# A recurrent cell on one core: three bf16 parts of h and its weights against one fp32 product in four column tiles

## What is computed

```
fused = sigmoid(concat([x_t, h]) @ w_W + w_b)
hidden_state, output_state = split(fused, 2)
memory_state = x_t @ wx_W + wx_b + hidden_state * (h @ wh_W + wh_b)
h_new = output_state * h + (1 - output_state) * tanh(memory_state)
```

## Time and profile before

| | |
|---|---|
| median of 3 runs | 2035.18 us (2035.16 to 2035.33) |
| the profiled execution | 2036.86 us |
| its span in the trace | 2032.7 us |
| PE busy | 1838.1 us, 90% of the span, 52224 matmul records |
| DVE busy | 1395.7 us, 69% |
| ACT busy | 1076.7 us, 53% |
| POOL busy | 271.1 us, 13% |
| mean granted TensorE clock | 0.997 of full speed |

### The profile page before, as it was taken

One profiled execution on the slowest core, in us unless ns is written; L12 is line 12 of the kernel. 1 busy time (PEld: TensorE's weight loads), 2 busy tenths in 40 slices (PEclk: granted clock), 3 DMA queues, 4 the chain that ended last, 5 costly groups with the idle time before them and its releaser, 6 DMA issues.

```text
span 2032.7 us, 127549 instructions
## 1 busy us (share of the span) xinstructions
PE 1838.1 (90%) x52224; PEld 1646.3 (81%) x52224; DVE 1395.7 (69%) x7191; ACT 1076.7 (53%) x5003; POOL 271.1 (13%) x1284
## 2 busy tenths in 40 slices
PE   5999999999999999999999999999999999999986
PEld 4888888888888888888888888888888888888875
DVE  6666666666666666666666666666666666666666
ACT  4555555555555555555555555555555555555544
POOL 0111111111111111111111111111111111111111
PEclk9999999999999999999999999999999999999989
DMA  5210000000000000000000000000000000000000
GB/s 177 81 45 9 9 9 8 4 8 9 9 9 3 9 8 9 9 8 4 9 8 9 9 5 7 9 8 9 9 3 9 8 9 9 8 4 9 8 9 9
DMA packets 35801, 30.00 MB, mean 15 GB/s; under 512 B 1584, under 2 KB 34352, under 8 KB 35376
## 3 DMA queue, kind: packets, MB, share of 16 engines
q1 hardware_dynamic: 35376, 23.10, 3.5%
HBM read 14.70 MB, written 8.39 MB: 11 GB/s over the span
## 4 chain that ended last, share of the span: by engine, by line
PE 71%; DVE 21%; issue 5%; DMA 1%; SPq 0%; POOL 0%; ACT 0%; POOLq 0%; DVEq 0%
PE ps L218 39%; PE ps L232 33%; DVE m_pre L377 5%; DVE h L397 5%; DVE h L392 5%; DVE h L386 4%; DVE pre_z L373 1%; DMA x_sb<-in_x 1%; PE ps L207 0%; SPq L183 0%; SPq L175 0%; DVE ps L365 0%; SPq L178 0%; POOL y L485 0%; DVE m_add L412 0%
## 5 line engine op out<-in xcount | busy, mean ns | idle before, releaser
L218 PE MATMUL ps<-wh,h 128*24 128x256 bf16 x24576 | 782.6, 276 | 166.3 <-DVE h L397 157.4
L218 PEld LDWEIGHTS ps<-wh,h 128*24 128x24 bf16 x24576 | 648.6, 123 | 261.7 <-DVE h L397 256.5
L232 PEld LDWEIGHTS ps<-h_moving,wh 128*128 128x128 bf16 x24576 | 649.3, 96 | 96.0 <-issue 96.0
L232 PE MATMUL ps<-h_moving,wh 128*128 128x24 bf16 x24576 | 698.9, 173 | 0.0
L365 DVE STREAM_TRANSPOSE ps<-ps 128x128 f32<-128x128 f32 x1024 | 271.2, 310 | 529.2 <-PE ps L218 529.2
L207 PE MATMUL ps<-x_sb,wx 128*128 (+1 forms) x3072 | 460.0, 289 | 22.4 <-DMA wx<-in_w_x 20.3
L306 ACT ACTIVATE m_by<-pre_r 128x32 f32<-128x32 f32 x512 | 133.9, 261 | 631.8 <-DVE pre_r L410 631.8
L301 ACT ACTIVATE h_moving<-h 128x48 bf16<-128x48 bf16 x1024 | 303.9, 297 | 246.3 <-DVE h L397 241.5
L472 POOL COPY m_add<-xg 128x16 f32 (+1 forms) x1024 | 186.6, 218 | 1724.1 <-DVE m_pre L377 1687.3
L207 PEld LDWEIGHTS ps<-x_sb,wx 128*128 128x128 f32 x3072 | 380.9, 192 | 22.8 <-issue 20.3
L290 ACT ACTIVATE h_by<-pre_z 128x16 f32<-128x16 f32 x1024 | 236.7, 231 | 52.4 <-DVE pre_z L373 1.2
(11 more groups left out here) (19 smaller groups left out, 122.3 us busy)
## 6 DMA issues: line engine op xcount, KB each, us to landing
x_sb<-in_x SPq DMA_DIRECT2D x32, 256.0 KB, 3.1
out_h<-y SPq DMA_DIRECT2D x32, 256.0 KB, 2.6
wh_rest<-in_w_h SPq DMA_DIRECT2D x4, 768.0 KB, 11.4
wx<-in_w_x SPq DMA_DIRECT2D x4, 768.0 KB, 11.8
h<-in_h SPq DMA_DIRECT2D x1, 16.0 KB, 1.8
bias_x<-in_b_x SPq DMA_DIRECT2D x1, 6.0 KB, 1.9
bias_h<-in_b_h SPq DMA_DIRECT2D x1, 2.0 KB, 1.7
```

Of the source, the lines that this page charges most:

```text
L218: mm = pe.matmul(ps[Q * j:Q * j + PARTS * B, RM_BANK, 0:RM], parts_of(s - 1 if s else S, k), wh[:, part, k, j * RM:(j + 1) * RM], start=(k ...
L232: mm = pe.matmul(ps[:, Z_BANK + o, ci * SLOTS * B:(ci * SLOTS + PARTS) * B], wh[:, part, k, col:col + P], h_moving[:, k // HC, k % HC, :], ...
```

## The change

h and its weights stay fp32. wh is loaded as it is, in one buffer; the cutting of the weights, the two subtractions on h, h_moving and the reductions over parts go away. Each chunk of h stands as 8 fp32 columns in each of the four column tiles. Two groups of products follow each other: r and m (256 moving columns, PSUM bank 0), then z (128 moving columns, bank 1), both by the one function products. Per step these are 16 + 16 matmuls in place of 48 + 48. z is now turned by a transpose as r and m are (turn_z). The sums of r and z with x's share are plain additions in SBUF; x's share is placed there by one copy on ACT (place_x), two buffers deep. GpSimd adds the bias to hm (hidden), and adds x to h in every step. The order on DVE becomes: both transposes of r and m, sums of r, both m scans, then z. At the start SP loads wx in six parts by unit, then wh, and the x products wait part by part.

```diff
...
-            for k in range(KC // 2):
-                load_wh(k)
+            sp.dma_start(x_sb[:, :, 0:TOK], x_flat[:, :, 0:TOK]).then_inc(x0_loaded, 16)
+            for i in range(WX_PARTS):
+                us = slice(i * UNITS // WX_PARTS, (i + 1) * UNITS // WX_PARTS)
+                sp.dma_start(wx[:, us], w_x[:, us]).then_inc(wx_loaded[i], 16)
+                if i == 0:
+                    sp.dma_start(bias_x[:, :], b_x).then_inc(bias_loaded, 16)
+                    sp.dma_start(bias_h[:, :], b_h).then_inc(bias_loaded, 16)
+                    sp.dma_start(h_0[:, :, :], h0).then_inc(h0_loaded, 16)
             for k in range(KC):
-                sp.dma_start(wx[:, k, :, :], w_x[:, k, :, :]).then_inc(wx_loaded, 16)
-            for k in range(KC // 2, KC):
-                load_wh(k)
+                sp.dma_start(wh[:, k], w_h[:, k]).then_inc(wh_loaded, 16)
+            sp.dma_start(x_sb[:, :, TOK:2 * TOK], x_flat[:, :, TOK:2 * TOK]).then_inc(x_loaded, 16)
...
-            def rm_products(ks, s):
-
...
-                    for part in range(PARTS):
-                        for j in range(TILES):
-                            mm = pe.matmul(ps[Q * j:Q * j + PARTS * B, RM_BANK, 0:RM],
-                                           parts_of(s - 1 if s else S, k),
-                                           wh[:, part, k, j * RM:(j + 1) * RM],
...
-            def z_products(o):
-
-                for ci in range(HC):
...
+            def products(group, half, s):
+
+
+                at, cols, bank = group
+                for k in range(half * HC, (half + 1) * HC):
+                    for j in range(TILES):
+                        mm = pe.matmul(ps[Q * j:Q * j + B, bank, 0:cols], h_of(s - 1 if s else S, k),
+                                       wh[:, k, j, at:at + cols], start=(k == 0), stop=(k == KC - 1),
+                                       tile_position=(0, Q * j))
                 return mm
 
             def step(t0, s):
                 nxt = held(pe, t0 + (s + 1))
                 pe.wait_ge(h_ready[0], nxt)
-                rm_products(range(HC), s)
+                products(RM, 0, s)
                 pe.wait_ge(h_ready[1], nxt)
-                rm_products(range(HC, KC), s).then_inc(rm_done, 1)
-                pe.wait_ge(h_moved, nxt)
-                pe.wait_ge(xz_placed, nxt)
-                for o in range(HALVES):
-                    z_products(o).then_inc(z_done[o], 1)
-
-            pe.wait_ge(x_loaded, 2 * 16)
-            pe.wait_ge(wx_loaded, KC * 16)
+                products(RM, 1, s).then_inc(rm_done, 1)
+                products(Z_ALL, 0, s)
+                products(Z_ALL, 1, s).then_inc(z_done, 1)
+            pe.wait_ge(x0_loaded, 16)
             x_products(x_list, 0, 0)
-            for k in range(KC):
-                pe.wait_ge(first_cut[k], 1)
-                pe.wait_ge(next_cut[k], PARTS - 1)
+            pe.wait_ge(wh_loaded, KC * 16)
             pe.wait_ge(ps_cleared, 1)
...
+            def place_x(which, s):
+                dst = add[:, s % 2].rearrange("p o g i w -> p (o g i) w")[:, :, 1]
+                act.activation(dst, xg[:, which, s].rearrange("p a u b -> p (a u b)"), ACT.Copy).then_inc(x_placed, 1)
+
+            def reset(o, nxt):
+                act.wait_ge(r_summed[o], nxt)
+                act.activation(m_by[:, o, :, 1], pre_r[:, o, :], ACT.Sigmoid).then_inc(r_ready[o], 1)
 
...
             def step(t0, s, this, other, unit0, last):
                 nxt = held(act, t0 + (s + 1))
-                act.wait_ge(r_summed, nxt)
-                act.activation(by_chunk(m_by, 1), pre_r[:, :, :].rearrange("p (o c) b -> p o c b", c=HC), ACT.Sigmoid)\
-                    .then_inc(r_ready, 1)
+                reset(0, nxt)
+                reset(1, nxt)
+                new(0, s, nxt)
+                new(1, s, nxt)
                 update(0, nxt)
-                new(0, s, nxt)
                 update(1, nxt)
-                new(1, s, nxt)
-                if s < S:
-                    place_xr(this, s + 1)
-                    place_xz(this, s + 1)
-                elif not last:
-                    place_xr(other, 0)
-                    place_xz(other, 0)
-                if s < S or not last:
-                    nxt2 = held(act, t0 + (s + 2))
-                    move_h(0, s, nxt2)
-                    move_h(1, s, nxt2).then_inc(h_moved, 1)
                 if not last:
                     for u in X_ENDS[s]:
                         empty(u, other, unit0)
-                    if s == S - 1:
-                        act.wait_ge(xg_ready, unit0 + UNITS)
-                        act.sem_inc(xg_turned, 1)
+                if s < S:
+                    place_x(this, s + 1)
+                elif not last:
+                    act.wait_ge(xg_ready, unit0 + UNITS)
...
+            def turn_rm(o):
+                dve.transpose(turned[:, o, R:Z].rearrange("p g c q -> p (g c) q"),
+                              ps[:, 0, o * P:(o + 1) * P].rearrange("p (c q) -> p c q", q=Q)).then_inc(rm_turned[o], 1)
+
+            def turn_z():
+                dve.transpose(turned[:, :, Z], ps[:, 1, 0:P].rearrange("p (o c q) -> p o c q", c=HC, q=Q))\
+                    .then_inc(z_turned, 1)
+
+            def sum_r(o, par, nxt):
+                dve.tensor_tensor(pre_r[:, o].rearrange("p (c b) -> p c b", b=B), product_of(o, R), x_of(par, o, R),
+                                  ALU.add).then_inc(r_summed[o], 1)
+
+            def sum_z(o, par, nxt):
+                dve.tensor_tensor(pre_z[:, o].rearrange("p (c b) -> p c b", b=B), product_of(o, Z), x_of(par, o, Z),
+                                  ALU.add).then_inc(z_summed[o], 1)
+
+            def mix_m(o, par, nxt):
+                dve.wait_ge(r_ready[o], nxt)
+                dve.wait_ge(hm_ready[o], nxt)
                 dve.tensor_tensor_scan(m_pre[:, o].rearrange("p i w -> p (i w)"),
                                        m_by[:, o].rearrange("p i w -> p (i w)"),
-                                       m_add[:, o].rearrange("p i w -> p (i w)"), 0.0, ALU.mult, ALU.add)\
+                                       add[:, par, o, M].rearrange("p i w -> p (i w)"), 0.0, ALU.mult, ALU.add)\
                     .then_inc(m_pre_ready[o], 1)
 
...
             def step(t0, i, s):
                 nxt = held(dve, t0 + (s + 1))
-                if s == 0:
-                    dve.wait_ge(y_early, held(dve, i + 1))
-                if s == Y_HALF:
-                    dve.wait_ge(y_late, held(dve, i + 1))
+                par = s % 2
+                if s % Y_HALF == 0:
+                    dve.wait_ge(y_added, held(dve, t0 + (s + Y_HALF)))
                 dve.wait_ge(rm_done, nxt)
-                dve.wait_ge(xr_placed, nxt)
-                turn(R, r_turned)
-                turn(M, m_turned)
-                dve.wait_ge(r_turned, nxt)
-                dve.tensor_reduce(pre_r[:, :, :], summed(R), AX.X, ALU.add).then_inc(r_summed, 1)
-                dve.wait_ge(m_turned, nxt)
-                dve.tensor_reduce(by_chunk(m_add, 0), summed(M).rearrange("p (o c) b s -> p o c b s", c=HC),
-                                  AX.X, ALU.add).then_inc(hm_summed, 1)
-                sum_z(0, nxt)
-                dve.wait_ge(r_ready, nxt)
-                dve.wait_ge(hm_summed, nxt)
-                dve.wait_ge(xm_placed, nxt)
-                mix_m(0)
-                sum_z(1, nxt)
-                mix_m(1)
+                turn_rm(0)
+                turn_rm(1)
+                dve.wait_ge(rm_turned[0], nxt)
+                dve.wait_ge(x_placed, nxt)
+                sum_r(0, par, nxt)
+                dve.wait_ge(rm_turned[1], nxt)
+                sum_r(1, par, nxt)
+                mix_m(0, par, nxt)
+                mix_m(1, par, nxt)
+                dve.wait_ge(z_done, nxt)
+                turn_z()
+                dve.wait_ge(z_turned, nxt)
+                sum_z(0, par, nxt)
+                sum_z(1, par, nxt)
                 mix_h(0, s, nxt)
-                write_rest1(0, s, nxt)
-                write_rest2(0, s, nxt)
                 mix_h(1, s, nxt)
-                write_rest1(1, s, nxt)
-                write_rest2(1, s, nxt)
-
...
+            def hidden(o, par, nxt):
+                pool.wait_ge(rm_turned[o], nxt)
+                pool.tensor_tensor(add[:, par, o, M, :, 0].rearrange("p (c b) -> p c b", b=B), product_of(o, M),
+                                   bias_h[:, HC * o:HC * (o + 1)].unsqueeze(2).to_broadcast([P, HC, B]), ALU.add)\
+                    .then_inc(hm_ready[o], 1)
+
...
+                pool.tensor_tensor(y[:, :, s, :].rearrange("p (o c) b -> p o c b", c=HC),
+                                   x_sb[:, :, cols].rearrange("p (o c) b -> p o c b", c=HC), hs, ALU.add)\
+                    .then_inc(y_added, 1)
+
+            def step(t0, s):
+                nxt = held(pool, t0 + (s + 1))
                 for o in range(HALVES):
```

(1 more changed line is left out.)

306 lines of the change are left out of this document (89 added, 217 removed).

## The result

| | before | changed |
|---|---|---|
| median | 2035.26 us (2035.16 to 2042.80, 4 runs) | 2264.26 us (2263.19 to 2266.77, 4 runs) |
| ratio, 95% interval | | 1.1121 [1.1107, 1.1135] |
| span in the trace | 2032.7 us | 2264.9 us |
| mean granted clock | 0.997 | 0.991 |
| usual step, first transpose to the next | 3.88 us | 4.30 us |

A forecast was written before the change was run, and what follows sets the result against it. It took each step as r and m on PE, then DVE and ACT, with z ending late after the change: 512 x 6.78 = 3471, + 22 + 6 + 3.7 + 4.2 - 1.7 = 3505 us; range 2230 to 3740.

The forecast's parts named there:

- The step that failed: PE's column tiles: starts in program order let two tiles work at a time, 0.218 us per 256-column product, step 6.78 us.
- rival (a): PE's column tiles: four work at a time, as in bf16; step 4.35 us, 2261 us in all; chance 0.10.
- fp32 costs four times bf16: PE's products: an fp32 product is two records of two passes each, four passes in all.
- The last r and m record: PE, with four tiles at a time: last r and m record starts at 1.57 us, DVE at 2.01.
- DVE's chain: DVE and ACT after r and m: 1.20 us until DVE is free for z, then 1.14 to PE.
- The removed subtractions: DVE's two subtractions per half of h: 0.22 us each with hand-over, 0.44 on the path.
- Ends: Outside the usual steps: first step at 22 us, 6 us on leaving the loop, 3.7 us after the last h.

The follow-up runs named there:

- e3: Changed kernel with all four chunks of a tile (eight records) in a row, both halves of h awaited first: 3807.19 us, 1.8692.
- e9: Kernel before with tile outside, then chunk, then weight part, so six matmuls of one tile in a row: 2624.59 us, 1.2881.
- e1: Kernel before with the two inner loops of r and m swapped, three weight parts of one tile in a row: 2063.06 us, 1.0129.
- e2: Changed kernel with tile outside and chunk inside within a half, four records of one tile in a row: 2293.07 us, 1.1258.
- e7: Changed kernel with the two waits ahead of the h scan in the other order: 2232.75 us, 1.0966.
- e4: Kernel before without the four subtractions that renew the second and third parts of h: 1872.46 us, 0.9193.
- e13: Changed kernel with SP's stores of results issued between its loads of x: 2239.3 us, 1.0987.
- e10: Kernel before with two bf16 parts of h and its weights in place of three: 1709.19 us, 0.8389.
- e15: Kernel before with its start alone changed: wx loaded in six parts, cutting in the order needed: 2030.54 us, 0.9971.
- e8: Changed kernel with r, m and z as three groups of 128 columns, each transposed by itself: 2222.46 us, 1.0918.
- e11: Changed kernel with r, m and z as three groups and both pairs of waits swapped: 2150.65 us, 1.0561.
- e12: Kernel before with r and m as two groups in two banks, m scans and tanh moved ahead, h scan's waits swapped: 2288.2 us, 1.1229.

## Why the prediction was wrong

- **The step that failed** is the one on the tiles: "low(j) waits for high(j), and high(j+1), standing behind it, starts only beside low(j). Two tiles work at a time, not four." The runs fit a queue per tile, in which one record streams and three wait; only a fifth for the same tile holds up what is behind (e3, and e9, forecast from it). The changed kernel puts two in a row, and two, three (e1) and four (e2) in a row still run four tiles at a time. So rival (a) held: 8 rounds of 0.216 us and not 16 of 0.218, with the last r and m record at 1.54 us and not 3.53, and a step of 4.30 and not 6.78. That all starts of before are in program order was no evidence: there neighbours are always in different tiles, and both rules give the same trace. I gave (a) 0.10, and the rows could not tell the two cases apart; an even split would have been the reading. The Trainium skill, TensorE: Matmul & The Clock Gate, Part 3: Packing small matmuls, says matmuls start strictly in program order: these runs disagree for starts in different column tiles, since with eight in a row (e3) the next tile's first starts ahead of three of the tile before. The fourfold overlap of TensorEngine Tiling (Array Packing), Theoretical Speedup, in the Trainium skill, agrees with the trace.
- **fp32 costs four times bf16**: right. A round of 256 columns takes 0.216 us for each of two records, in bf16 0.109 for one; a round of 128 takes 0.109. The bounds were 0.218 to 0.223 and 0.109 to 0.122. The loads of 8 fp32 columns take 90 ns and lengthen no round.
- **The last r and m record** in case (a): 1.57 forecast; by rounds (0.02 + 0.22 + 6 x 0.216) it is 1.54. DVE starts at 1.99 for 2.01.
- **DVE's chain**: 1.20 to z's transpose and 1.14 from it to PE were forecast. It was 1.14 and 1.18: 2.32 for 2.34. From the sigmoid's start to the h scan I had put 0.28; it took 0.32, and 0.26 with the waits in the other order (e7).
- **The removed subtractions** were worth 0.44 on the path. e4 confirms 0.36 before PE becomes the bound. By the timeline the changed kernel lost as much by moving z behind the m scans, which the sum for (a) held.
- **Ends**: first step at 21.42 for 22; end of the last h to the end of the span 3.5 for 3.7; the slow steps on leaving the loop 5.8 for 6.
- **Missing**: the 30 us at step 17 were in no term. The y add in every step had none, but it moved the first need of a store from step 24 to step 16, at 21.4 + 17 x 4.3 = 94.5 us, while SP's queue issues no store before 121.77; before, step 24 comes at 37.8 + 24 x 3.88 = 131, when the first store has been issued (at 124.62). GpSimd's own queue took the m scan along. e13 shows it by taking it away. In the kernel before the same wait appears as soon as the steps or the start are earlier: step 25 took 9.95 us in e4, 8.98 in e10 and 9.49 in e15.
- **(a)'s 2261 us** is 3 us off in part by luck: the step was 0.05 too long (24 us) and the stall of 30 us was missing.

## What to carry to other kernels

Where column tiles stand beside each other, what counts is how many matmuls of one tile follow in a row: three (bf16) and four (fp32) cost 1.3%, six and eight made the tiles wait for each other. For a recurrence take the cost of a step from the path PE to DVE to ACT and back: a smaller sum of busy time (DVE 380 us less) bought nothing here, as PE's first group took longer and z moved behind m. When an engine's extra work begins to need a DMA, look at what stands ahead of that DMA in its queue: the first few dozen steps can hide a stall that no average shows.

## What was not expected of the hardware

- Each column tile takes four matmuls (one streaming, three waiting) before the queue's head blocks (e3: the second tile starts with the fifth of eight records; e9: with the third of six).
- The order in which two waits are written ahead of one instruction of DVE, the one released last first or second: 0.06 us a step (e7), and with the m scan's pair as well 0.13 (e8 to e11).
- A tile's first round in bf16 takes 0.147 us and not 0.109 (e9); in fp32 it takes 0.223 and not 0.216 in the changed kernel, but 0.215 in the first tile of e3.
- Rounds of 128 bf16 columns take 0.056 us, but in 247 of 512 steps the 96 products have a pause over 0.12 us that no other engine's work explains, at places some 256 instructions apart (e12).
- TensorE's granted clock fell to half in the stall of the changed kernel (mean 0.56 from 100 to 115 us, with no matmul running), and the first products behind it took 5.31 us instead of 2.79.
